# Graph attention and mixture of experts on one core: router logits computed with nodes on partitions late in the low products, one wait per tile for the one-hots, and the first stage's scores made by ScalarE

## The reference

```python
h = norm(x) @ W + b_w                       # 2500 x 512
e = leaky_relu(s_dst[dst] + s_src[src] + b_a, 0.2)   # s_dst = h @ a[:512], s_src = h @ a[512:]
w = exp(e); alpha = w / segment_sum(w, dst)[dst]
x = x + segment_sum(alpha[:, None] * h[src], dst)
n = norm(x)
logits = n @ Wg + bg                        # 2500 x 8
comb = softmax(logits), kept where it is among the 2 largest
x = x + sum over e of comb[:, e] * (gelu(n @ W1[e] + b1[e]) @ W2[e] + b2[e])
```

## Time and profile before

| | us |
|---|---|
| median of 3 runs (lowest, highest) | 787.21 (786.38, 789.01) |
| the profiled execution's own time | 787.67 |
| span of the profiled execution | 786.0 |
| TensorE busy in it | 701.5 |
| VectorE busy in it | 559.3 |
| ScalarE busy in it | 458.8 |
| mean granted TensorE clock (1 is full) | 0.954 |

### The profile page before, as it was taken

One profiled execution on the slowest core, in us unless ns is written; L12 is line 12 of the kernel. 1 busy time (PEld: TensorE's weight loads), 2 busy tenths in 40 slices (PEclk: granted clock), 3 DMA queues, 4 the chain that ended last, 5 costly groups with the idle time before them and its releaser, 6 DMA issues.

```text
span 786.0 us, 15439 instructions
## 1 busy us (share of the span) xinstructions
PE 701.5 (89%) x3556; PEld 527.0 (67%) x3557; DVE 559.3 (71%) x1520; ACT 458.8 (58%) x1226; POOL 283.5 (36%) x427
## 2 busy tenths in 40 slices
PE   3977863999899999999999999999589899999992
PEld 1855641777677776767677777776347788888881
DVE  4999977999888898879887888853495333333331
ACT  3223379778778776767676777721354455555551
POOL 3336620022222222222111222211305677777764
PEclk9888976999999999999999999999789999999998
DMA  9431000000000000000000000000793577777766
GB/s 337 158 107 55 0 1 1 15 29 28 28 27 3 28 27 28 27 28 27 28 27 28 27 12 17 27 28 28 245 407 112 103 130 133 133 128 135 135 119 80
DMA packets 28949, 59.70 MB, mean 76 GB/s; under 512 B 3664, under 2 KB 8144, under 8 KB 28624
## 3 DMA queue, kind: packets, MB, share of 16 engines
q0 software_dynamic: 10176, 24.12, 17.1%
q1 hardware_dynamic: 18704, 34.89, 12.0%
HBM read 35.93 MB, written 23.07 MB: 75 GB/s over the span
## 4 chain that ended last, share of the span: by engine, by line
PE 52%; DMA 10%; issue 5%; DVE 4%; POOL 2%; POOLq 2%; ACT 0%; DVEq 0%; ACTq 0%
PE ps L772 10%; PE ps L790 10%; PE ps L773 9%; DMA out_dram<-y,si 9%; PE ps L726 7%; PE ps L879 3%; PE ps L753 2%; PE ps L893 2%; PE ps L737 2%; PE ps L820 1%; DMA xg<-xn_table,gi 1%; PE ps L746 1%; PE ps L869 1%; PE ps L759 1%; DVE hot_r L1509 1%
## 5 line engine op out<-in xcount | busy, mean ns | idle before, releaser
L973 ACT ACTIVATE weight<-sdst_b,ss 128x125 f32 (+1 forms) x400 | 118.3, 386 | 95.5 <-DVE A_lo L1339 95.5
L772 PE MATMUL ps<-H_hi,A_hi 128*125 128x512 f32 x400 | 163.0, 408 | 0.9 <-DVE x_all L1353 0.9
L773 PE MATMUL ps<-H_lo,A_hi 128*125 128x512 f32 x400 | 157.9, 395 | 0.0
L1278 DVE TENSOR_SCALAR hot_k<-lane_k,key_t 128x250 bf16<-128x250 bf16 x600 | 120.6, 282 | 4.4 <-DVE weight_sum L1327 4.3
L524 POOL TENSOR_SCALAR seed<-seed 128x1 f32<-128x1 f32 x20 | 4.2, 210 | 330.9 <-DVE seed L1380 330.9
L982 ACT ACTIVATE weight<-weight,ss 128x125 f32<-128x125 f32 x400 | 119.8, 384 | 0.0
L790 PE MATMUL ps<-H_hi,A_lo 128*125 128x512 f32 x400 | 104.9, 402 | 0.0
L726 PE MATMUL ps<-hot_k,hot_l 128*128 128x250 bf16 x500 | 80.7, 286 | 16.0 <-DVE hot_k L1278 15.9
L772 PEld LDWEIGHTS ps<-H_hi,A_hi 128*125 128x125 f32 x400 | 74.2, 185 | 21.6 <-issue 3.7
L773 PEld LDWEIGHTS ps<-H_lo,A_hi 128*125 128x125 f32 x400 | 74.3, 186 | 16.1
L879 PE MATMUL ps<-W_e,xgT 128*128 x352 | 85.0, 385 | 0.0
(11 more groups left out here) (235 smaller groups left out, 1126.7 us busy)
## 6 DMA issues: line engine op xcount, KB each, us to landing
W_e<-in_L_ffn_W_dram SPq DMA_DIRECT2D x16, 512.0 KB, 9.3
xf<-in_x_cols_dram SPq DMA_DIRECT2D x10, 512.0 KB, 5.9
x_all<-in_x_dram SPq DMA_DIRECT2D x20, 256.0 KB, 5.8
out_dram<-x_all SPq DMA_DIRECT2D x20, 256.0 KB, 2.0
xn_table<-xn SPq DMA_DIRECT2D x20, 256.0 KB, 2.2
b_b<-in_L_ffn_b_dram SPq DMA_DIRECT2D x1, 2048.0 KB, 12.6
Wf<-in_L_gnn_W_dram SPq DMA_DIRECT2D x1, 1024.0 KB, 5.5
out_dram<-x_all POOLq DMA_DIRECT2D x4, 256.0 KB, 7.8
```

The source lines that it names most:

```text
L772: pe.matmul(ps_agg[0:TN, :], A_hi[:, k, :], H_hi[:, k, :], start=(k == 0), stop=False)
L773: m = pe.matmul(ps_agg[0:TN, :], A_hi[:, k, :], H_lo[:, k, :], start=False, stop=False)
L973: m = nc.scalar.activation(weight[:, s, k, :], dst_scores, ACT.Relu, bias=ss[:, 0, k:k + 1], scale=1.0 - SLOPE)
L1278: return nc.vector.tensor_scalar(into, lane_k[:, :], float(HW * h), key, ALU.add, ALU.is_equal)
```

## The change

- The logits are made in one step with nodes on partitions: for each of 4 slices the transposed rows (128 x 128) are the stationary operand and `Wg` (8 columns) is the moving one, straight into `ps_nodes`. They stand after product 15 of the low part. `logits_of_nodes`, `logT_of`, the tile `logT` and its semaphores are gone. The bias is loaded to all partitions (`bg_b`) and added by VectorE once, for all tiles, before the softmax.
- In the loop's steps TensorE waits once for all 10 halves' one-hots of a tile; in the steps written out it waits for each half as before.
- VectorE's `reciprocal_of` goes ahead of all 30 one-hots.
- `s_dot` is gone: ScalarE makes each tile's column of `ss` and `s_dst` from `s_raw` with 1/std as its scale (4 instructions), and a fifth makes the row for 0.2. The factor 0.8 moves from the `relus` to the `exps`. VectorE's 1/std of step `u` waits for the scores of step `u - 2`, a wait that stood behind the dot products of step `u`.

```diff
@@ count
+                at_once = not isinstance(t, int)
+                if at_once:
+                    pe.wait_ge(pairs_ok, HALVES * t + HALVES)
                 for h in range(HALVES):
-                    pe.wait_ge(pairs_ok, HALVES * t + h + 1)
+                    if not at_once:
+                        pe.wait_ge(pairs_ok, HALVES * t + h + 1)
@@ normal_T
-                    pe.wait_ge(logT_ok, t)
+                    pe.wait_ge(xnT_ok, t)
@@ logits
                 for k in range(KT):
-                    m = pe.matmul(ps_T[0:NX, 0:P], Wg_sb[:, k, :], xnT[:, k, :], start=(k == 0), stop=(k == KT - 1))
-                m.then_inc(logT_ps, 1)
-
-            def logits_of_nodes(t):
-
-                pe.wait_ge(logT_ok, t + 1)
-                pe.matmul(ps_nodes[:, bass.ds(t * NX, NX)], logT[:, :], ident[0:NX, 0:NX], start=True, stop=True)\
-                    .then_inc(logit_ps, 1)
+                    m = pe.matmul(ps_nodes[:, bass.ds(t * NX, NX)], xnT[:, k, :], Wg_sb[:, k, :],
+                                  start=(k == 0), stop=(k == KT - 1))
+                m.then_inc(logit_ps, 1)
@@ tile_products
-                        if k == NT // 4 and has(t, 3):
-                            logits(t - 3)
...
-                        if k == NT // 4 and has(t, 3):
-                            pe.wait_ge(den_ok, t + 1)
-                            logits_of_nodes(t - 3)
                         if k == NT // 2 and has(t, 2):
                             normal_T(t - 2, s)
+                        if k == 3 * NT // 4 and has(t, 3):
+                            pe.wait_ge(den_ok, t + 1)
+                            logits(t - 3)
@@ scores (ScalarE)
-                act.wait_ge(dot_ok, u + 1)
-                for k in range(2):
-                    m = nc.scalar.activation(ss[:, k, 2 * u:2 * u + 2], s_dot[:, s, 0, :], ACT.Identity,
-                                             bias=cst3[:, k:k + 1], scale=(1.0 - SLOPE, SLOPE)[k])
+                act.wait_ge(raw_ok, 4 * u + 4)
+                for j in range(2):
+                    m = nc.scalar.activation(ss[:, 0, 2 * u + j:2 * u + j + 1], s_raw[:, s, 0, j:j + 1], ACT.Identity,
+                                             bias=cst3[:, 0:1], scale=rstd[:, s, j:j + 1])
                 m.then_inc(s_ok, 1)
...
+                act.wait_ge(s_ok, u + 1)
+                nc.scalar.activation(ss[:, 1, 2 * u:2 * u + 2], ss[:, 0, 2 * u:2 * u + 2], ACT.Copy, scale=SLOPE)\
+                    .then_inc(s_low_ok, 1)
@@ xnT_of (ScalarE)
-                    act.wait_ge(logT_ps, t)
+                    act.wait_ge(logit_ps, t)
@@ rstd_of (VectorE)
                 dve.wait_ge(std_ok, u + 1)
+                if u >= 2:
+                    dve.wait_ge(s_dst_ok, u - 1)
@@ node_rows (VectorE)
-                dve.wait_ge(raw_ok, 4 * u + 4)
-                if u >= 2:
-                    dve.wait_ge(s_dst_ok, u - 1)
-                nc.vector.tensor_tensor(s_dot[:, s, :, :], s_raw[:, s, :, :],
-                                        rstd[:, s, :].unsqueeze(1).to_broadcast([P, 2, 2]), ALU.mult).then_inc(dot_ok, 1)
@@ tile_step (VectorE)
+                if here:
+                    reciprocal_of(t, s)
                 if has(t, -2):
...
-                    pairs_of(t + 2, at, range(0, HALVES // 2))
-                if here:
-                    reciprocal_of(t, s)
-                if has(t, -2):
-                    pairs_of(t + 2, at, range(HALVES // 2, HALVES))
+                    pairs_of(t + 2, at, range(HALVES))
@@ softmax (VectorE)
-            link(V.tensor_reduce(red[:, :], logit, AX.X, ALU.max))
+            link(V.tensor_tensor(score[:, :, :], logit, bg_b[:, :].unsqueeze(1).to_broadcast([P, NT, NX]), ALU.add))
+            link(V.tensor_reduce(red[:, :], score[:, :, :], AX.X, ALU.max))
```

More of the change, by code:

```diff
@@ L78, in gnn_moe_kernel @@
         xnT = sb("xnT", [P, KT, P], F32)
-        logT = sb("logT", [NX, P], F32)
         Wg_sb = sb("Wg_sb", [P, KT, NX], F32)
-        bg_c = sb("bg_c", [NX, 1], F32)
+        bg_b = sb("bg_b", [P, NX], F32)
         start = sb("start", [P, 5], F32)
@@ L152, in gnn_moe_kernel @@
         s_raw = sg("s_raw", [P, 2, 2, 2], F32, first)
-        s_dot = sg("s_dot", [P, 2, 2, 2], F32, first)
         s_dst = sg("s_dst", [P, NT], F32, first)
@@ L295, in gnn_moe_kernel @@
         H_hi_ok, H_lo_ok = sem("H_hi_ok"), sem("H_lo_ok")
-        raw_ok, dot_ok, s_ok, s_dst_ok = sem("raw_ok"), sem("dot_ok"), sem("s_ok"), sem("s_dst_ok")
+        raw_ok, s_ok, s_low_ok, s_dst_ok = sem("raw_ok"), sem("s_ok"), sem("s_low_ok"), sem("s_dst_ok")
         mm_ok, mm_ps, span_ok, found_ok, found_ps, early_ok, table_ok = (sem(n) for n in (
@@ L314, in gnn_moe_kernel @@
         minus_ok = sem("minus_ok")
-        xnT_ps, xnT_ok, logT_ps, logT_ok, logit_ps = (sem(n) for n in (
-            "xnT_ps", "xnT_ok", "logT_ps", "logT_ok", "logit_ps"))
+        xnT_ps, xnT_ok, logit_ps = (sem(n) for n in ("xnT_ps", "xnT_ok", "logit_ps"))
         shift_ok, exp2_ok, cnt_ok, cnt_ps = sem("shift_ok"), sem("exp2_ok"), sem("cnt_ok"), sem("cnt_ps")
@@ L417, in _ @@
             sp.dma_start(Wg_sb[:, :, :], Wg.rearrange("(k p) e -> p k e", p=P)).then_inc(ld_late, 16)
-            sp.dma_start(bg_c[:, :], bg.rearrange("(e o) -> e o", o=1)).then_inc(ld_late, 16)
+            sp.dma_start(bg_b[:, :], bg.partition_broadcast(P)).then_inc(ld_late, 16)
             sp.dma_start(chunk_d[:, :, :], dst_chunks[:, :, :]).then_inc(ld_edge, 16)
@@ L783, in tile_products @@
                                 .then_inc(den_ps, 1)
-                elif has(t, 3):
-                    logits(t - 3)
                 if has(t, 0):
@@ L931, in scores @@
             def scores(u, s):
-                act.wait_ge(dot_ok, u + 1)
-                for k in range(2):
-                    m = nc.scalar.activation(ss[:, k, 2 * u:2 * u + 2], s_dot[:, s, 0, :], ACT.Identity,
-                                             bias=cst3[:, k:k + 1], scale=(1.0 - SLOPE, SLOPE)[k])
+                act.wait_ge(raw_ok, 4 * u + 4)
+                for j in range(2):
+                    m = nc.scalar.activation(ss[:, 0, 2 * u + j:2 * u + j + 1], s_raw[:, s, 0, j:j + 1], ACT.Identity,
+                                             bias=cst3[:, 0:1], scale=rstd[:, s, j:j + 1])
                 m.then_inc(s_ok, 1)
-                nc.scalar.activation(s_dst[:, 2 * u:2 * u + 2], s_dot[:, s, 1, :], ACT.Identity, bias=cst3[:, 2:3])\
-                    .then_inc(s_dst_ok, 1)
+                for j in range(2):
+                    m = nc.scalar.activation(s_dst[:, 2 * u + j:2 * u + j + 1], s_raw[:, s, 1, j:j + 1], ACT.Identity,
+                                             bias=cst3[:, 2:3], scale=rstd[:, s, j:j + 1])
+                m.then_inc(s_dst_ok, 1)
+                act.wait_ge(s_ok, u + 1)
+                nc.scalar.activation(ss[:, 1, 2 * u:2 * u + 2], ss[:, 0, 2 * u:2 * u + 2], ACT.Copy, scale=SLOPE)\
+                    .then_inc(s_low_ok, 1)
             def high_rows(u, s):
@@ L972, in relus @@
                 for k in range(NT):
-                    m = nc.scalar.activation(weight[:, s, k, :], dst_scores, ACT.Relu, bias=ss[:, 0, k:k + 1],
-                                             scale=1.0 - SLOPE)
+                    m = nc.scalar.activation(weight[:, s, k, :], dst_scores, ACT.Relu, bias=ss[:, 0, k:k + 1])
                     if k % (NT // 2) == NT // 2 - 1:
@@ L981, in exps @@
                 for k in range(part * NT // 2, (part + 1) * NT // 2):
-                    m = nc.scalar.activation(weight[:, s, k, :], weight[:, s, k, :], ACT.Exp, bias=ss[:, 1, k:k + 1])
+                    m = nc.scalar.activation(weight[:, s, k, :], weight[:, s, k, :], ACT.Exp, bias=ss[:, 1, k:k + 1],
+                                             scale=1.0 - SLOPE)
                 if part == 1:
@@ L1028, in tile_weights @@
                         high_weights(t + 1, 1 - s, q)
-                if has(t, 3):
-                    logT_of(t - 3)
                 if has(t, -2):
@@ L1039, in _ @@
             act.wait_ge(d_ok, len(ps_d))
-            act.wait_ge(s_ok, NT // 2)
+            act.wait_ge(s_low_ok, NT // 2)
             act.wait_ge(ld_late, 16 * 2)
@@ L1169, in _ @@
             link(nc.vector.tensor_tensor(s_bias[:, 0:1], s_bias[:, 0:1], ba_b[:, :], ALU.add))
-            for k in range(2):
-                m = nc.vector.tensor_scalar(cst3[:, k:k + 1], s_bias[:, 0:1], (1.0 - SLOPE, SLOPE)[k], None, ALU.mult)
-            m.then_inc(cst_ok, 1)
+            nc.vector.tensor_copy(cst3[:, 0:1], s_bias[:, 0:1]).then_inc(cst_ok, 1)
             dve.wait_ge(ld_edge, 48)
@@ L1451, in _ @@
             logit = ps_nodes.rearrange("p (t e) -> p t e", e=NX)
-            link(V.tensor_reduce(red[:, :], logit, AX.X, ALU.max))
-            V.tensor_tensor(score[:, :, :], logit, bc_t(red[:, :]), ALU.subtract).then_inc(shift_ok, 1)
+            link(V.tensor_tensor(score[:, :, :], logit, bg_b[:, :].unsqueeze(1).to_broadcast([P, NT, NX]), ALU.add))
```

(2 more changed lines are left out.)

## The result

The changed kernel takes 768.13 us (median of 4 runs, 766.5 to 768.55) against 786.87 for the kernel before (4 runs, 786.38 to 789.01). The ratio is 0.9753, with a 95% interval of 0.973 to 0.9776. The prediction was 765.3, from 755 to 774. The profiled execution took 767.86 us, its span is 766.2.

A forecast was written before the change was run, and what follows sets the result against it. It took TensorE's chain to bound the loop before, VectorE after. First stage 2.0, steps 0 to 3 1.9, loop 15.1, steps 18 and 19 1.6, end 1.3: 21.9 us off 787.67, so 765.3 at the median; range 755 to 774.

The forecast's parts named there:

- Logits, 0.79 us a tile: TensorE's low products: old logits cost 1.66 us a tile, the eight new passes 0.87, so 0.79 goes.
- One wait, 0.92 us (0.68 to 1.17): TensorE's pair counting in the loop: dropping the computed waits saves 0.92 us a step on its sequencer.
- The word load, exposed by 0.3 us more a step (0 to 0.6): TensorE's sequencer: eight short passes queued make the 2.63 us load start later, costing 0.3 us a step.
- VectorE sets it, not TensorE: Loop: VectorE's work and jump set a round of 40.8 us; TensorE's own would be 40.2.
- my first rival: Loop: TensorE stays the bound by its sequencer, round 41.5 to 42, time 770 to 773; chance 0.15.
- my third rival: Loop: VectorE's rounds hide more, jump's gap included; round falls to TensorE's 39.6, time 757; chance 0.1.
- the countings: Sign in the profile after: TensorE's countings in the loop at 3.1 to 3.4 us.
- the jump on the chain: Sign in the profile after: the 2.8 us of VectorE's loop jump lie on the chain of waits.
- Around the loop: Outside loop steps 4 to 17: steps 0 to 3 give 1.9 us, 18 and 19 give 1.6, the end 1.3.
- First stage, 2.0 (0 to 8): Stage before attention, set by VectorE: dropping `s_dot` gains 2.0 us, bounds 0 and 8.
- The rival in which all stalls are given: First stage: VectorE saves 8 us or more if TensorE's and ScalarE's work moves up; 757; chance 0.15.
- The slower rival: Loop: logits passes break the product stream; at 0.4 us a pass +8 us, 796; chance 0.03.

The follow-up runs named there:

- the last kernel but one in the table: Changed kernel with TensorE's word load before the last pair of high products, and VectorE's 14 loop steps written out: 753.39 us, ratio 0.9573 to before.
- the kernel with the load before the last pair: Changed kernel with TensorE's word load for the next tile's counting made before the last pair of high products: 759.25 us, ratio 0.9653 to before.
- the early logits: Changed kernel with the logits after low product 5 in place of 15, nothing else: 761.0 us, ratio 0.9669 to before.

## Why the prediction was right, and where it was not

- **Logits, 0.79 us a tile: right.** 0.75 measured. That the load of 128 stationary columns is not added to a short product also holds: with both in it, a pass takes 0.10 us. The formula of "TensorE: Matmul & The Clock Gate" of the Trainium skill, section "LDWEIGHTS (loading the stationary operand)", gives an estimate of 0.107 us for such a load; the trace agrees with it as the whole price of a pass, and not as an addition.
- **One wait, 0.92 us (0.68 to 1.17): right.** 0.86 us on the sequencer's path, 0.79 in the loop's time when undone.
- **The word load, exposed by 0.3 us more a step (0 to 0.6): mis-sized.** It is 0.66, outside my bounds, and this is the term that failed. I had the mechanism (short passes in the queue in place of products), but took the size from a difference between two kinds of step that no run ties to it. With the three measured terms TensorE's own round is 42.97 - 2 x 0.75 - 2 x 0.86 + 2 x 0.66 = 41.07 us; 41.13 is measured, and I had 40.2.
- **"VectorE sets it, not TensorE": wrong.** VectorE alone needs 39.9 us a round, and I had 40.8. I left the jump's 2.80 us as they were, while with the reciprocal's new place 2.08 are left of them; in the other direction the new place itself saves 0.15 us a step and not 0.3. So the bound is the one of my first rival (chance 0.15), TensorE's sequencer, at 41.17 instead of its 41.5 to 42, and VectorE's rounds hide the jump as my third rival (0.1) had it. The forecast's range for the round (40.3 to 41.3) held the result for the wrong reason, and that is luck: TensorE's round came out 0.9 us above my figure for it and so ended just 0.4 us above the figure that I had put down to VectorE. In the 14 steps that is 2.4 us. The other stretches gave 0.35 us more than forecast, so that the profiled executions differ by 19.8 us where I had 21.9; the median of the runs is 2.8 us above the likeliest time.
- **Signs that failed:** the countings (3.54 us, not 3.1 to 3.4), VectorE no longer waiting for the last low product, and the jump on the chain. The round of 41.17 alone would not have shown it.
- **What I didn't see:** the wait for `den_ok` at L759 inside the loop. I named it for step 3 only. It would have taken 8 of the 13 us that wait and reciprocal give; the change happens to remove it, by the reciprocal's new place and by the logits' new form. That is luck as well.
- **Around the loop:** steps 18 and 19 gave 0.67 in place of 1.6, for the same exposed load (step 18 is not shorter at all); steps 1 to 3 gave 2.6 for 1.9. The tail's 1.33 is right, VectorE's bias add took 0.33 us where I put 0.36.
- **First stage, 2.0 (0 to 8): near.** 2.95 came in the two profiled executions, 2.25 with this part alone. VectorE waits for ScalarE in two of the ten steps. How the gain is made up of single stalls was not tested. The rival in which all stalls are given falls, though not for the new wait alone: without that wait TensorE and GpSimd hold the stage, and nothing more comes.
- **The slower rival** would have needed 0.33 us a pass; 0.10 is measured.

## What to carry to other kernels

An engine with no idle time can still be held by its sequencer. Ask for each wait, load of registers and jump how far the sequencer has run ahead when it gets there, and put the slow ones (here 2.63 us for a tile's words) where the lead is longest, behind a run of long instructions and not behind short ones. And test the parts of a change in pairs too: the one wait alone gave 4.9 us, the reciprocal's place adds 8.2 to it, and neither number is to be had from the other.

## What was not expected of the hardware

- A wait costs lead before it costs idle time. "Perfetto Trace Analysis" of the Trainium skill, section "Sequencer-only Instruction (DRAIN, etc)", has the sequencer itself wait for the semaphore and fetch the next instruction only afterwards. The loop's countings of the last kernel but one in the table agree: 2.88 us where the one-hots ended 1.4 to 1.5 us ahead of the last low product, 3.47 to 3.55 us where they ended 0.15 to 0.4 us ahead, without idle time ahead of these 25 products.
- How bare a jump lies depends on what stands ahead of it: 2.9 to 3.3 us of idle time with a series of 15 behind the reciprocal, 2.0 to 2.3 with one of 30 instructions. Without VectorE's jump the kernel with the load before the last pair gained 5.9 us. "Runtime: NRT & Kernel Launch", section "Instruction fetch mechanics", of the Trainium skill names such a stall as a reason to write loops out; these runs agree for VectorE, the only engine whose loop was written out. Whether the jump's target lay outside what had been fetched ahead, which is the page's condition, no run shows.
- Why the lead shrinks behind the eight short passes stays open: the queue may hold so many instructions and short ones last less long, or the sequencer may need longer to hand out 16 instructions than TensorE to run them. No run here tells these apart; both say that ten products behind them restore it, as the early logits show.
